# Gathers of a graph kernel in pairs: the second of a pair waits until the pair ahead has landed

## The reference

```
m_in     = concat([x[src], x[dst], edge_attr])     # 400000 x 144
h        = silu(m_in @ W1 + b1)                    # 400000 x 64
messages = silu(h @ W2 + b2)                       # 400000 x 64
agg      = segment_sum(messages, dst)              # 12500 x 64
out      = layernorm(x + silu(concat([x, agg]) @ W3 + b3))
```

## Time and profile before

| | |
|---|---|
| median of 3 runs | 3711.9 us (3711.58 to 3713.22) |
| the profiled execution, its own time | 3709.15 us |
| its span, first to last instruction | 3707.2 us |
| instructions | 51553 |
| PE busy | 2939.1 us, 79% |
| PE weight loads | 2072.0 us, 56% |
| DVE busy | 2573.0 us, 69% |
| ACT busy | 1080.7 us, 29% |
| POOL busy | 2777.4 us, 75% |
| mean granted TensorE clock | 0.889 of full speed |
| gathers' DMA queue (q0) | 93856 packets, 96.30 MB, 11.8% of 16 engines' span |
| SP's DMA queue (q1) | 232774 packets, 54.48 MB, 7.1% |

### The profile page before, as it was taken

The page is one execution under the profiler, slowest core; times in us unless marked ns, Lnnn a source line. Parts: engine busy times, 40 slices in busy tenths (PEclk is TensorE's granted clock), DMA queues, the critical chain, the costliest instruction groups (busy, mean ns, idle before and its releaser), DMA issues.

```text
span 3707.2 us, 51553 instructions
## 1 busy us (share of the span) xinstructions
PE 2939.1 (79%) x15108; PEld 2072.0 (56%) x15108; DVE 2573.0 (69%) x5725; ACT 1080.7 (29%) x1687; POOL 2777.4 (75%) x2943
## 2 busy tenths in 40 slices
PE   3898788887877878778878787888787888888875
PEld 2666555555555555555555555555555555555553
DVE  7788667666676766666667676666666666676664
ACT  1333223222232322323223232232323223232222
POOL 7777777777777777777777777777777777777774
PEclk9999889898898888888888889988988888898887
DMA  7121121111111121111111211121111211111111
GB/s 168 36 46 35 37 46 37 39 35 43 40 37 39 35 47 35 37 40 41 42 35 37 46 37 40 35 46 36 37 39 35 48 35 37 39 41 42 34 30 27
DMA packets 328736, 154.48 MB, mean 42 GB/s; under 512 B 215582, under 2 KB 281151, under 8 KB 328470
## 3 DMA queue, kind: packets, MB, share of 16 engines
q0 software_dynamic: 93856, 96.30, 11.8%
q1 hardware_dynamic: 232774, 54.48, 7.1%
q10 hardware_dynamic: 1840, 0.34, 0.1%
HBM read 141.26 MB, written 9.62 MB: 41 GB/s over the span
## 4 chain that ended last, share of the span: by engine, by line
POOL 67%; issue 22%; DVE 5%; PE 3%; DMA 1%; POOLq 1%; ACT 0%; DVEq 0%; ACTq 0%; SPq 0%
POOL edge_in L489 67%; PE pick_ps L1082 1%; DVE pair L782 1%; DVE masked L777 1%; DVE every L775 1%; PE z_ps L1047 1%; DVE z_ps L764 0%; DMA node_terms<-lot_T 0%; DMA edge_in<-in_x_dram,src_i 0%; DVE rows_T L814 0%; DVE edge_in L750 0%; PE pick_ps L1014 0%; PE in_ps L1023 0%; PE agg_ps L1060 0%; POOLq L508 0%
## 5 line engine op out<-in xcount | busy, mean ns | idle before, releaser
L489 POOL DMA_INDIRECT edge_in<-in_x_dram,src_i x2933 | 2776.2, 947 | 895.6 <-issue 890.3
L1082 PE MATMUL pick_ps<-parts,rows_T 128*128 128x512 f32 (+1 forms) x4992 | 1569.3, 444 | 0.0
L1082 PEld LDWEIGHTS pick_ps<-parts,rows_T 128*128 128x128 f32 x4992 | 955.5, 211 | 483.0 <-issue 311.6
L1023 PE MATMUL in_ps<-ident,edge_in 128*128 128x128 f32 x3128 | 503.7, 314 | 606.4 <-DMA edge_in<-in_x_dram,src_i 606.3
L1023 PEld LDWEIGHTS in_ps<-ident,edge_in 128*128 128x128 f32 x3128 | 404.4, 161 | 702.5 <-issue 550.1
L569 ACT COPY in_T<-in_ps 128x1024 f32<-128x1024 f32 x391 | 395.8, 1012 | 1179.3 <-PE in_ps L1023 1163.6
L577 ACT ACTIVATE z_ps<-z_ps,zero_col 128x512 f32<-128x512 f32 x391 | 258.8, 662 | 1162.4 <-DVE z_ps L764 1162.4
L764 DVE TENSOR_TENSOR z_ps<-z_ps,b_rep 128x512 f32<-128x512 f32 x391 | 271.6, 695 | 433.0 <-PE z_ps L1047 432.1
L1047 PEld LDWEIGHTS z_ps<-w_bd,h_T 128*128 128x128 f32 x3128 | 468.8, 221 | 28.2
L1047 PE MATMUL z_ps<-w_bd,h_T 128*128 128x128 f32 x3128 | 471.2, 300 | 0.0
L1041 PE MATMUL z_ps<-in_T,w_in 128*64 128x512 f32 x782 | 422.6, 622 | 1.2 <-ACT in_T L569 1.2
(11 more groups left out here) (101 smaller groups left out, 1540.1 us busy)
## 6 DMA issues: line engine op xcount, KB each, us to landing
edge_in<-in_x_dram,src_i POOLq DMA_INDIRECT x2933, 2.4
ea<-in_edge_attr_dram SPq DMA_DIRECT2D x48, 512.0 KB, 4.5
w_in<-node_terms SPq DMA_DIRECT2D x391, 12.0 KB
node_terms<-h_T SPq DMA_DIRECT2D x12, 256.0 KB, 2.4
node_terms<-lot_T SPq DMA_DIRECT2D x12, 256.0 KB, 2.3
y<-in_x_dram SPq DMA_DIRECT2D x15, 192.0 KB
term<-node_terms SPq DMA_DIRECT2D x15, 192.0 KB
out_dram<-y SPq DMA_DIRECT2D x15, 192.0 KB, 2.3
```

The source lines that it names most:

```text
L489: pool.indirect_dma_start(out=edge_in[:, to_slot, t, XS], out_offset=None, in_=x[:, :], in_offset=bass.IndirectOffsetOnAxis(ap=indices[:, ...
L1023: last = nc.tensor.transpose(in_ps[:, t // HT, t % HT * P:(t % HT + 1) * P], edge_in[:, s, t, :], ident[:, :])
L1082: last = nc.tensor.matmul(pick_ps[r][:, 0:(b - a) * H], rows_T[:, i % 2, c, :], parts[:, j, a:b, :].rearrange("p k f -> p (k f)"), start=( ...
```

## The change

The tiles of a group are taken as pairs: (0,1), (2,3), (4,5), (6,7). The first three pairs have a semaphore each (`s_pair_of_x[0..2]`); the last pair of every group counts on one semaphore for all slots, `s_xg`. Ahead of the second tile of a pair POOL now waits until the pair ahead has landed: for tiles 3, 5 and 7 the pair before in the same group, for tile 1 the last pair of the group before. In groups with seven gathers tile 7 and its wait don't exist, and the last pair is tile 6 alone. PE waits for `s_xg` instead of the slot's semaphore; `rows_landed` now sums the last pairs of all groups up to this one. The five gathers of the last group have one wait ahead of the first. The number of gathers, their form, their order and all else stay.

```diff
+    PAIRS = T // 2
+    LAST_PAIR = T - 2
+
+    def last_of(g):
+        return tiles_of(g) if g == FULL else tiles_of(g) - LAST_PAIR
+
-    def rows_landed(k, v):
+    def rows_landed(k, v, bodies=range(1, BODIES)):
         def upto(g):
-            return sum(tiles_of(h) for h in range(g % S, g + 1, S))
+            return sum(last_of(h) for h in range(g + 1))
         if isinstance(k, int):
             return 16 * upto(k * B + v)
...
-        s_xg = [sem(f"x_gathered{s}") for s in range(S)]
+        s_pair_of_x = [sem(f"x_pair_gathered{j}") for j in range(PAIRS - 1)]
+        s_xg = sem("x_gathered")
...
             def fill(k, v, tiles):
                 q, column_of = ring(v)
                 if column_of == 0:
                     pool.wait_ge(s_src[q], loaded(k, v))
                     pool.nop(nofuse=True)
-                gather(src_i[:, q, column_of, :], v % S, tiles, s_xg[v % S])
+                for t in range(tiles):
+                    pair, second = t // 2, t % 2
+                    if second and pair:
+                        pool.wait_ge(s_pair_of_x[pair - 1], k * (32 * B) + 32 * (v + 1))
+                        pool.nop(nofuse=True)
+                    elif second and not (isinstance(k, int) and k * B + v == 0):
+                        pool.wait_ge(s_xg, rows_landed(k, v - 1, TURNS))
+                        pool.nop(nofuse=True)
+                    gather_tile(src_i[:, q, column_of, :], v % S, t, s_xg if t >= LAST_PAIR else s_pair_of_x[pair])
...
                 pool.wait_ge(s_in_T, FULL - S + 1)
                 pool.wait_ge(s_tail, 16)
-                gather(src_i[:, ring(FULL)[0], FULL % CH, :], FULL % S, TT, s_xg[FULL % S])
+                pool.wait_ge(s_xg, rows_landed(0, FULL - 1))
+                gather(src_i[:, ring(FULL)[0], FULL % CH, :], FULL % S, TT, s_xg)
...
-                pe.wait_ge(s_xg[v % S], rows_landed(k, v))
+                pe.wait_ge(s_xg, rows_landed(k, v))
```

More of the change, by code:

```diff
@@ L108, in tiles_of @@
         return TT if g == FULL else T - picked(g)
-    def rows_landed(k, v):
+    PAIRS = T // 2
[3 more added lines that the diff above has]
+    def rows_landed(k, v, bodies=range(1, BODIES)):
         def upto(g):
-            return sum(tiles_of(h) for h in range(g % S, g + 1, S))
+            return sum(last_of(h) for h in range(g + 1))
         if isinstance(k, int):
             return 16 * upto(k * B + v)
-        each = upto(2 * B + v) - upto(B + v)
-        assert all(upto(q * B + v) == upto(B + v) + (q - 1) * each for q in range(1, BODIES) if q * B + v < FULL)
-        return k * (16 * each) + 16 * (upto(B + v) - each)
+        one, two, *_ = bodies
+        each = upto(two * B + v) - upto(one * B + v)
+        assert all(upto(q * B + v) == upto(one * B + v) + (q - one) * each for q in bodies if q * B + v < FULL)
+        return k * (16 * each) + 16 * (upto(one * B + v) - one * each)
     ctx = ExitStack()
@@ L485, in _, with gather_tile @@
                            allow_small_or_imprecise_dtypes=True).then_inc(s_const, 1)
-            def gather(indices, to_slot, tiles, arrived):
-                for t in range(tiles):
+            def gather_tile(indices, to_slot, t, arrived):
                     pool.indirect_dma_start(
@@ L492, in gather @@
                     ).then_inc(arrived, 16)
+            def gather(indices, to_slot, tiles, arrived):
+                for t in range(tiles):
+                    gather_tile(indices, to_slot, t, arrived)
+            TURNS = range((FULL - S) // B)
             def fill(k, v, tiles):
@@ L510, in refill @@
                     fill(k, v, tiles)
-                turns = (FULL - S) // B
+                turns = len(TURNS)
                 with pool.Fori(0, turns) as k:
@@ L968, in any_group @@
                         nc.vector.tensor_add(window, window, agg_ps[H:P, 0:P]).then_inc(a_added, 1)
-                for s in range(S):
-                    dve.wait_ge(s_xg[s], 16 * tiles_of(s))
+                dve.wait_ge(s_xg, rows_landed(0, S - 1))
                 nc.vector.memset(edge_in[:, SRC:DST + 1, :, :], 0.0).then_inc(a_clear, 1)
```

## The result

| | before | after |
|---|---|---|
| median of 4 runs | 3711.74 us (3707.49 to 3713.22) | 4778.38 us (4773.84 to 4796.41) |
| ratio, 95% interval | | 1.2885 (1.2848 to 1.2922) |
| profiled execution, own time | 3709.15 us | 4773.86 us |
| first gather to start of the last | 4.0 to 3672.9 | 4.0 to 4740.7 |
| mean granted TensorE clock | 0.889 | 0.790 |

The change makes the kernel slower by 1067 us, or 29%. The stretch of the gathers alone grows from 3668.9 to 4736.7, by 1067.8, so all of it lies there; what comes after the last gather even gets 3 us shorter (31.3 instead of 34.3). Over 1368 waits that is 0.78 us a wait.

The account below looks back on a forecast made before the run. The prediction took POOL's gather line as the bound. 623 us for some 1328 waits, 10 for chunk loads and 40 for the first 110 us made 673 on top of 3709.2: 4380 us, range 3830 to 4800.

Parts of the forecast that it names:

- The bound: POOL's gather line: a gather every 1.249 us, POOL waiting for nobody, so any delay of a gather moves the end equally.
- The start-up: On POOL, from the end of an unmet wait to the held gather's recorded start: 0.51 us, between 0.30 and 0.72.
- Landing and waking: From a gather's start to its last semaphore increment, mean 2.417 us; then until POOL's wait ends, 0.04 us.
- the 10 us for chunk loads: Added to the sum for long landings beside SP's chunk loads, where the view mostly gives no landing.
- The first part: The first 110 us: about 18 us for early slow landings, then 22 for some 30 waits, together 40 us.
- B: Rival: POOL's start-up before second tiles is hidden or short, 0.2 us or less; 3820 us, up to 3930; chance 0.18.
- C: Rival: the first gather's cold start-up of 0.87 us holds at every wait, POOL falling asleep between pairs; 4870 us; chance 0.15.
- D: Rival: not slower, landing plus start-up fitting in two gather intervals at second tiles; 3702 to 3716 us; chance 0.05.

Follow-up runs that it names:

- all three distances: All eight tiles gathered, waits for gathers begun two, three or four gather intervals (1.25 us each) earlier: 5221.15, 4053.42 and 3994.36 us, against 3944.90 without waits.
- three beats: Kernel with all eight tiles gathered, plus a wait ahead of each pair's first tile for the pair two ahead (3.75 us): 4053.42 us against 3944.90.
- the kernel of one beat: Changed kernel with the wait for the pair just ahead moved from the second tile of a pair to the first, 1559 waits: 6893.97 us.
- one wait a group: Kernel with all eight tiles gathered, plus a wait at tile 1 for the whole group ahead, 389 waits: 4373.38 us against 3944.90 without waits.
- four beats: Kernel with all eight tiles gathered, plus a wait ahead of each pair's second tile for the pair two ahead (5.0 us): 3994.36 us against 3944.90.
- all tiles gathered: Kernel before with PE's picking of an eighth tile removed, 3125 gathers instead of 2933: 3944.90 us without waits, 5221.15 with the change's waits.

## Why the prediction was right, and where its sum fell short

**The bound, and what the waits do.** POOL held the end, so that each us at a gather came out at the end: right, 1067.8 in the stretch against 1067 in the time. A gather's own 0.944 stayed, the landing stayed, the waits are handled right ahead of their gather instead of twelve ahead: as predicted. 0.30 ahead of first tiles and 0.6 to 1.0 ahead of second ones was said; 0.30 came, and a median of 0.94 ahead of second ones. POOL's share is 58%, not 64%, since the span is longer. The forecast was 4380 in a range of 3830 to 4800; 4778 is near its upper end, and the added time, 1067 us, is 1.6 times the 668 that was said.

**The start-up is the term that failed.** "The nearest rows are the two of the gather itself, 0.30 and 0.72; between them I take the middle, 0.51." It is 0.72. That is 0.21 x 1328 = 279 us of the 395 by which the sum was short (1068 in the stretch against 673). The prediction had the right number in hand as the upper end, 0.87 less the 0.15 by which the cold gather is longer than a warm one, and gave 4650 for it. Nothing in the trace spoke for a value between the two rows: 0.30 is measured with the next gather lying ready in the queue, the very thing that a wait takes away, and the first gather, however cold, was the only row in which a gather came behind an unmet wait. The row of the same situation should have been taken, not the middle.

**Landing and waking** were 2.417 and 0.04; the chain shows 2.29 to 2.45 and 0.05, and all landings behind the waits have a mean of 2.45. Right.

**The long pieces** were the second miss. The turn of the loop (29 us) and the piece at every 107 to 109 gathers (60) weren't in the prediction at all. Late landings were: they are in its mean landing of 2.417 and in the 10 us for chunk loads, and the measured mean of 2.45 makes 36 more. With 8 for the first part, 279 + 89 + 36 + 8 = 412; some 17 of it come back, since behind a long piece at a first tile the next landing has already passed. The prediction took POOL's queue as it was and asked only for the price of the waits. That 1368 waits also make POOL's program longer, so that the turn of the loop brings a fetch that the kernel before doesn't have, it didn't ask.

**The first part** was right. Eight gathers take from 4.03 to 27.73 and the ninth starts at 29.87, with long pieces behind landings of 8 us and more; 18 were said for it. The timeline's start, which answers to the earlier trace rows:

```profile
14.78 0.94 POOL L498 DMA_INDIRECT edge_in<-in_x_dram,src_i  x1 [7.16 <-DMA edge_in<-in_x_dram,src_i]
...
23.57 1.09 POOL L498 DMA_INDIRECT edge_in<-in_x_dram,src_i  x1 [6.60 <-DMA edge_in<-in_x_dram,src_i]
```

The 92nd gather starts at 169.33 instead of 121.8: 47.5 for the first part, where 40 stood.

**The whole sum again, with what was measured:** 1328 waits at 3.13 - 2.50 = 0.63 are 837 (landing 2.36, the middle of those in the chain), the first part 47.5, the long pieces 167; together 1051 of 1068. The other 17 are the spread of the pieces below 1.5 us.

**The rivals.** B, a short start-up, is out: the 0.30 isn't the closing of a gather with the next at once behind it. So is the figure that leaned that way: the Trainium skill (GPSIMD Engine Reference, section Performance versus the Vector engine) has 156 ns of dispatch for an instruction of the vector engine, and more hops for GpSimd; an indirect gather behind an unmet wait takes 0.72 here. C, the cold value each time, is out too: 0.72 stands behind nearly every wait, and not 0.87; but its time of 4870 lies nearer to the measured 4778 than the forecast of 4380. D would have needed landing and start-up within 2.46; they are at 3.12. The advice to issue early and wait late (the Trainium skill, DMA: Bandwidth & Descriptors, section Rules for kernel authors) agrees with all three distances: late enough here is three beats.

**PE** runs at a lower granted clock after the change, 0.790 against 0.889, and is busy for 3336.1 us instead of 2939.1 with the same instructions, while it waits for rows more than twice as long. With the chain on the gathers throughout, this didn't enter the time.

## What to carry to other kernels

Compare what a wait on the issuing engine needs, landing plus waking plus start-up (here 2.35 + 0.05 + 0.72 = 3.12 us), with the time until that engine would reach the held instruction anyway: below it each wait costs the difference, above it only late landings and POOL's own long pieces cost. Take the start-up from a row in which the engine stands behind an unmet wait, not from the gap between instructions that lie ready. And when a wait takes away the lead of a queue, list all that this lead hid: late landings of other loads' making, and work that the engine does now and then. Waits are instructions too: look at the instruction packets at the loop's turn before and after, since a longer body can bring a fetch that wasn't there.

## What the runs showed of the hardware that was not expected

- The start-up of an indirect gather on POOL behind an unmet wait is ordinarily 0.72 us wherever it was looked at: in the changed kernel, in the kernel of one beat and with one wait a group, behind different lines. Behind a wait that is met in good time it is not seen (0.32 at four beats).
- At each turn of a loop of 367 POOL instructions, two packets of instructions and 2.25 to 2.59 us of idle time ahead of the next gather; with 235 or 274 instructions there is no packet and no such piece.
- A long piece on POOL at a fixed count of gathers: start-ups of 3.35 us at every 108th gather with four waits a group and all tiles gathered (28 times), of 1.57 at every 32nd with one wait a group (94 times). In the kernels without waits no gather shows it. Its cause is open.
- The same kernel before took 3709 to 3712 us on the chips of most comparisons and 4690 on another, where the kernel with one wait a group has waits in its chain whose releaser the trace doesn't name. That is open too.
